# A branch hint on TensorE's layer-1 loop in a two-layer graph network

## The reference

```python
h = jnp.maximum(_layernorm(x, axis=-1), 0.0)
x = x + _L0_gnn_ref(h, edge_index, edge_attr_64, W1, b1, W2, b2)
h = jnp.maximum(_layernorm(x, axis=-1), 0.0)
x = x + _L1_gnn_ref(h, src, dst, w_neigh, w_self, b_self)
```

```python
summed = jax.ops.segment_sum(feat[src], dst, num_segments=n)
h_neigh_raw = summed / jnp.maximum(deg, 1.0)[:, None]
rst = feat @ w_self.T + b_self + h_neigh_raw @ w_neigh.T
```

## Time and profile before

| | |
|---|---|
| median of 3 runs | 1234.58 us (1234.28 to 1235.24) |
| the profiled execution's own time | 1235.77 us |
| its span, first to last instruction | 1234.0 us |
| TensorE matmuls busy | 1129.4 us (92%) |
| VectorE / ScalarE / GpSimd busy | 820.3 / 517.9 / 422.8 us |
| mean granted TensorE clock | 0.962 |

### The profile page before, as it was taken

How to read it: one execution, slowest core, us unless ns; L and a number is a source line. 1 busy time by engine, 2 the same in 40 slices (tenths; PEclk the granted TensorE clock), 3 DMA queues, 4 the chain that set the end, 5 groups by cost and what they waited for, 6 DMA issues and landing times.

```text
span 1234.0 us, 32065 instructions
## 1 busy us (share of the span) xinstructions
PE 1129.4 (92%) x11708; PEld 873.3 (71%) x11708; DVE 820.3 (66%) x1811; ACT 517.9 (42%) x982; POOL 422.8 (34%) x384
## 2 busy tenths in 40 slices
PE   2658999999997998599999999999999999999997
PEld 1657888888886887477777767767777776776774
DVE  3657687878786365676667767666666676675761
ACT  3681233333232244444444444444444444444441
POOL 3001111110110664064444534635434444462451
PEclk9875999999999898699999999999999999999999
DMA  3885444444446121121121211212212122121221
GB/s 112 297 276 171 143 136 137 144 137 141 130 141 195 48 73 41 35 74 56 56 70 56 74 52 54 72 51 72 60 54 70 54 64 60 55 77 51 62 69 38
DMA packets 67034, 115.87 MB, mean 94 GB/s; under 512 B 10644, under 2 KB 30824, under 8 KB 66962
## 3 DMA queue, kind: packets, MB, share of 16 engines
q1 hardware_dynamic: 51922, 75.12, 19.5%
q0 software_dynamic: 15040, 39.80, 11.5%
HBM read 101.93 MB, written 12.95 MB: 93 GB/s over the span
## 4 chain that ended last, share of the span: by engine, by line
PE 74%; DVE 6%; DMA 5%; issue 5%; POOL 3%; DVEq 3%; ACT 2%; SPq 0%; ACTq 0%; POOLq 0%
PE bank L1113 34%; PE couples L1106 9%; PE bank L1132 7%; PE couples L941 7%; PE bank L913 4%; PE bank L923 4%; POOL kreg L570 3%; PE bank L911 3%; DMA kreg<-in_edge_attr_dram 2%; PE bank L1124 2%; PE couples L946 1%; PE bank L1144 1%; DMA hreg<-in_dst_dram 1%; DMA kreg<-in_src_dram,startu 1%; DVE oreg L1543 1%
## 5 line engine op out<-in xcount | busy, mean ns | idle before, releaser
L1113 PE MATMUL bank<-hreg,areg 128*128 128x512 f16 x2058 | 505.1, 383 | 0.0
L588 POOL DMA_INDIRECT wide<-h_table,aggn x280 | 325.6, 1163 | 401.2 <-PE couples L1106 232.5
L770 ACT ACTIVATE areg<-couples 128x784 bf16<-128x784 f32 x336 | 276.7, 824 | 377.2 <-PE couples L1106 373.8
L1113 PEld LDWEIGHTS bank<-hreg,areg 128*128 128x128 bf16 x2058 | 265.8, 144 | 104.9 <-issue 1.6
L1543 DVE TENSOR_TENSOR hids<-iota,kreg 128x1024 bf16<-128x1024 f16 x336 | 196.8, 627 | 49.2 <-PE couples L1106 48.0
L1543 DVE TENSOR_TENSOR oreg<-iota,kreg 128x1024 bf16<-128x1024 f16 x336 | 196.1, 625 | 46.0 <-PE couples L1106 45.1
L941 PE MATMUL couples<-oreg,kreg 128*64 128x48 f32 x3232 | 147.2, 239 | 39.7 <-DVE oreg L1297 18.5
L941 PEld LDWEIGHTS couples<-oreg,kreg 128*64 128x64 f32 x3232 | 127.1, 152 | 67.4 <-issue 49.1
L555 POOL TENSOR_TENSOR xr<-xr,b2bc 128x512 f32 x25 | 32.6, 1306 | 306.1 <-ACT h0buf L674 306.1
L1297 DVE TENSOR_TENSOR oreg<-iota,wide 128x384 f32<-128x384 f32 x202 | 123.3, 611 | 6.2 <-issue 3.3
L1106 PEld LDWEIGHTS couples<-oreg 128*128 128x128 bf16 x1344 | 76.7, 98 | 52.5 <-DVE oreg L1543 13.7
(11 more groups left out here) (165 smaller groups left out, 1080.9 us busy)
## 6 DMA issues: line engine op xcount, KB each, us to landing
kreg<-in_edge_attr_dram SPq DMA_DIRECT2D x202, 256.0 KB, 2.8
h_table<-hreg SPq DMA_DIRECT2D x25, 256.0 KB
xr<-in_x_dram SPq DMA_DIRECT2D x6, 1024.0 KB, 6.6
out_dram<-hbuf SPq DMA_DIRECT2D x42, 128.0 KB
wide<-h_table,aggn POOLq DMA_INDIRECT x280
wide<-in_L_gnn_W_dram SPq DMA_DIRECT2D x2, 512.0 KB, 5.6
out_dram<-h0buf SPq DMA_DIRECT2D x6, 128.0 KB
hreg<-in_dst_dram SPq DMA_DIRECT2D x1, 512.0 KB
```

The source lines that it names most:

```text
L588: pool.indirect_dma_start(near[:, k, :], None, table, bass.IndirectOffsetOnAxis(ap=nearsrc[:, n * GHALF + k:n * GHALF + k + 1], axis=0)).t ...
L770: act.activation(step.rearrange("p (a k) -> p a k", a=2), cpl[s % 2][:, :, 0:BC * KEYS], ACT.Copy).then_inc(s_adj, 1)
L1113: ins = pe.matmul(bank[4 + par], adj[:, par, :, h], htab[:, h, :], start=(h == 0), stop=(h == TN - 1))
```

## The change

```diff
@@ -1184,7 +1184,8 @@
                 tile(0, 0, first=True)
                 for c in range(1, CYCLE):
                     tile(0, c)
-                with pe.Fori(1, GT - 1) as i:
+
+                with nc.Fori(1, GT - 1, engines=[mybir.EngineType.PE], hint_back_edge=True) as i:
                     for c in range(CYCLE):
                         tile(i, c)
                 for c in range(CYCLE):
```

## The result

The changed kernel is slower: 1239.45 us in the median of its 11 runs, against 1235.24 us for the kernel before beside it, ratio 1.0044 (95% interval 1.0026 to 1.0062), which is 5.4 us with an interval of 3.2 to 7.7; the two medians are 4.2 us apart. The forecast was 1234.7 us and no change.

A forecast was written before the change was run, and what follows sets the result against it. TensorE's matmuls, busy 92% of the span, were taken as the bound. No gain at the jumps and 0.1 us for the hint, added to the runs' median of 1234.58, gave 1234.7 us; range 1233.6 to 1236.4.

The forecast's parts named there:

- What bounds the kernel, and the jumps back: Layer-1 loop: TensorE's matmuls set the end; no jump back fetches or stalls, so the hint gains 0 for 4 jumps.
- Rival (a): Layer-1 loop's jumps back: they do stall and the hint removes it, 15.5 us faster, 1219.1 us; chance 2%.
- The hint's own cost: Head of each pass: one added instruction of 0.12 us, 5 in all, mostly hidden; 0 to 0.6 us, put at 0.1.
- the cover: Head of a pass: time from the end of L1103's wait to L1106's first weight load, 0.1 to 0.2 us.
- The room at the end of the block: Behind the loop's end: 0 to 48 instructions before a block crossing; one or two more use it up, chance about 1 in 15.
- The transfer that the hint starts: Head of each pass: the target is already there, so nothing moves, or a 16 KB packet a pass, 5 costing nothing.
- Rival (c): Loop exit: the hint pushes out the block behind the loop, one miss of 4.08 us, 1238.7 us; chance 3%.
- Rival (b): Head of each pass: eviction or a shifted block boundary makes four jumps stall, 15.1 us slower, 1249.7 us; chance 9%.

The follow-up runs named there:

- shift_only: Changed kernel with the hint replaced by one no-operation at the head of each pass; ratio 0.9996 to the kernel before.
- slot0_hint: Changed kernel, hint kept at the head, with the loop's first instruction loaded at slot 0 of a fetch block; ratio 1.0009 to the kernel before.
- late_hint: Changed kernel with the hint moved ahead of the last burst of a pass; ratio 1.0028 to the kernel before, 1.0015 when run once more.
- mid_hint: Changed kernel with the hint moved to the head of the fifth dense tile, 34 us before the pass ends; ratio 1.0039 to the kernel before.
- double_hint: Changed kernel with a loop body two passes long, hint at its head, and pass 5 written out; ratio 0.9999 to the kernel before.
- slot128_plain: Changed kernel without the hint, the loop's first instruction loaded at slot 128 of a fetch block; ratio 1.0147 to the kernel before.
- after_again: The changed kernel itself, run once more against the kernel before; ratio 1.0057.
- after: The changed kernel, with the hint at the head of each pass, against the kernel before; 1239.45 us, ratio 1.0044.

## Why the prediction was wrong

**What bounds the kernel, and the jumps back: right.** No jump stalled before, and none does after; the passes did not change by 0.1 us. The step from L1144 to L1106 at the first jump stays 1.19 to 1.20 us. Rival (a) had 2% and did not come.

**The hint's own cost: right.** One instruction of 31 to 55 ns a pass. It takes 0.09 us of the sequencer's time, where 0.12 was estimated, and is inside the cover: the loop lasts 504.7 us in both kernels, so the term of 0.1 us measured 0.0.

**The room at the end of the block: right in its use, and misused.** Between 0 and 48 instructions were worked out, and shift_only shows that one more did no harm. The same number was the condition of what did happen: with eleven instructions at hand the missing block stalls the array, with 65 (slot0_hint) it does not. The prediction looked at the room only for the shift.

**The transfer that the hint starts: the step that failed.** "Its target is the block that the engine is in at that moment. If the prefetcher sees that it has it, nothing moves. If it fetches it again, the cost as a transfer is a packet". Nothing did move, and that was the loss. The two cases that the prediction weighed left out a third: that the request for the target stands in place of another one. The earlier trace rows and the sixth packet of the earlier trace rows showed that a request for the block behind was made in the first pass and used in the last; the step never asked what the hint does to it. What stood in its place is the swap: no packet for the block behind in the first pass, one at 1120.1 us, 1.4 us behind the last branch, and 4.15 us lost there. It also took the hint to act where it stands; it acts where the branch's block is entered (late_hint, mid_hint, double_hint).

**Rival (c) named the place and nearly the price, with 3%.** One miss at the exit, 4.08 us: the stall and the clock behind it cost 4.15 us in the profile, and 1238.7 us stands beside a measured 1239.45, of which 0.7 us is the slower kernel before of that comparison. Its cause, a block pushed out, was wrong: no packet was loaded that could do it. Its evidence against, "the same as in (b)", was about eviction, so the case was given no weight of its own. That the price is so near is luck: it was to be 4.08 us of the sequencer's waiting, and it was 2.4 us of idle array and 1.8 us of lower clock.

**Rival (b): its premise was true, its sign for this change not.** The memory had no room to spare: one block more in the body costs 4.2 us a jump (slot128_plain). But the hint takes a block away from what must be held, and so removes that stall rather than making it.

The measured median lies 3.05 us above the range's upper end. The 5.4 us of the ratio have an interval of 3.2 to 7.7 us, so the 4.15 of the exit with SyncE's 0.4 lie within it, and the remaining 0.9 us is not resolved. The last products at the lower clock are seen in both profiles of this kernel (1.6 us here, 0.9 in after_again), but they come and go in kernels without the stall as well, and the doubt of 1 to 3 us named above comes on top.

## What to carry to other kernels

A prefetch hint is paid by the request that it replaces. Before adding one, find in the trace whether the jump stalls at all (a branch row of some 0.2 us does not, one of 3 to 4 us does), and what comes after the loop's last jump: with a hint, the code behind the exit is asked for only at the exit, and some 4 us of work (an estimate from the packet's 1.4 us and the 2.4 to 2.9 us until its code runs) must stand between the branch and the end of its fetch block, or the exit stalls once. The hint pays where the body and one block more do not fit in the engine's instruction memory; where a body just fits, its place within the fetch blocks decides 1.5% of this kernel's time, so look at the count of instruction packets over a pass whenever code ahead of such a loop changes length.

## What the runs showed of the hardware

- TensorE's instruction memory holds eight blocks of 16 KB: a body of seven and the one behind stay (no packet in four passes), eight and the one behind don't (nine packets a pass, and 3.3 to 3.9 us for each jump).
- A jump to a block that is there takes the sequencer 0.21 us, hidden behind a queue full of matmuls; one to a missing block 3.3 to 4.1 us.
- A hint costs 31 to 55 ns and stays armed for at least 192 us. It acts when the block of its branch is entered, in place of the request for the next block. If the branch falls through, the next block's packet starts 1.4 to 1.6 us later and its code runs 2.4 to 2.9 us after that.
- Idle stretches of 2.4 to 3.0 us at the exit (after, after_again, mid_hint) were each followed by a fall of TensorE's clock from 2.4 to 1.2 GHz for some 3.4 us, which cost 1.7 to 1.8 us more, three quarters on top of the stall where that was 2.4. It is not certain for each stall: in slot128_plain the clock fell behind three idle stretches (3.24, 2.73 and 2.77 us) and not behind the fourth (2.95 us).
- The end of the kernel can cost 0.9 to 1.7 us more when the clock falls before the last products are done, with or without a hint.
